# Preparation and attention as one unrolled program, with paired query tiles and an AV product shared by four heads

## The reference, cut to what matters

```
x = x + _layernorm(attention(_layernorm(x)))
x = x + _layernorm(moe(_layernorm(x)))

q = (x @ Wq.T) as 16 heads of 128;  k, v = 4 heads of 128 each
q, k = rope(q), rope(k);  each k and v head serves 4 q heads
scores = q @ k.T / sqrt(128), causal mask, softmax
out = (attn @ v).reshape(B, S, 2048) @ Wo.T
```

## Time and profile before

| what | us |
|---|---|
| median of 3 runs (2512.63 to 2517.93) | 2516.22 |
| span of the profiled execution, first to last instruction | 2515.8 |
| PE busy / weight loads / DVE / ACT / POOL | 2040.1 / 1825.9 / 1578.2 / 1186.3 / 715.7 |
| share of the span: PE / DVE / ACT / POOL | 81% / 63% / 47% / 28% |
| chain that ended last, as far as the page follows it | DVE 2% (the norm of `finish`) |

### The profile page before, as it was taken

One profiled execution on the slowest core, in us unless ns is written; L12 is line 12 of the kernel. 1 busy time (PEld: TensorE's weight loads), 2 busy tenths in 40 slices (PEclk: granted clock), 3 DMA queues, 4 the chain that ended last, 5 costly groups with the idle time before them and its releaser, 6 DMA issues. The chain is left out here.

```text
span 2515.8 us, 46912 instructions
## 1 busy us (share of the span) xinstructions
PE 2040.1 (81%) x15459; PEld 1825.9 (73%) x15459; DVE 1578.2 (63%) x3449; ACT 1186.3 (47%) x2906; POOL 715.7 (28%) x760
## 2 busy tenths in 40 slices
PE   1269999999989999998999999899999747636630
PEld 1159999989879998887899989789998625434420
DVE  5237676766877766688676767876676548810008
ACT  2026566656556666555566656556666411111110
POOL 0012332323323333223333323333333100034542
PEclk9969999999999999999999999999999957756655
DMA  9600101020110001011100020110100022145535
GB/s 371 261 17 26 43 2 43 2 76 18 43 52 26 18 27 40 38 43 51 44 15 29 1 77 18 43 51 26 43 1 1 1 91 74 42 142 130 132 98 183
DMA packets 71749, 153.57 MB, mean 61 GB/s; under 512 B 9496, under 2 KB 52392, under 8 KB 67928
## 3 DMA queue, kind: packets, MB, share of 16 engines
q1 hardware_dynamic: 62840, 126.60, 14.6%
q0 software_dynamic: 8672, 24.02, 3.5%
HBM read 106.34 MB, written 44.26 MB: 60 GB/s over the span
## 5 line engine op out<-in xcount | busy, mean ns | idle before, releaser
L387 PE MATMUL s_ps<-kT,qT 128*128 128x512 f32 (+3 forms) x2304 | 577.0, 367 | 23.3 <-PE prod_ps L353 9.2
L568 ACT ACTIVATE pT<-t_ps 128x512 fp32r<-128x512 f32 (+3 forms) x768 | 349.3, 491 | 390.6 <-PE t_ps L396 387.4
L408 PE MATMUL av_ps<-pT,v 128*128 128x256 f32 (+1 forms) x3840 | 502.3, 283 | 19.8 <-ACT y_part L584 17.0
L408 PEld LDWEIGHTS av_ps<-pT,v 128*128 128x128 f32 x3840 | 472.7, 191 | 34.8 <-issue 18.7
L493 DVE TENSOR_REDUCE neg_max<-s_ps 128x1 f32<-128x128 f32 (+7 forms) x512 | 385.5, 753 | 126.0 <-PE s_ps L387 117.8
L387 PEld LDWEIGHTS s_ps<-kT,qT 128*128 128x128 f32 x2304 | 406.7, 194 | 66.2 <-issue 31.9
L560 ACT ACTIVATE probs<-s_ps,neg_max 128x128 f32<-128x128 f32 (+7 forms) x512 | 381.7, 746 | 120.8 <-DVE neg_max L493 119.5
L500 DVE TENSOR_TENSOR pT<-t_ps,pT 128x512 fp32r<-128x512 f32 (+3 forms) x768 | 400.9, 549 | 25.9 <-ACT pT L568 19.5
L616 POOL TENSOR_TENSOR roped<-rope_c,rope_s 128x256 f32<-128x256 f32 (+1 forms) x192 | 124.2, 647 | 972.6 <-DVE rope_s L483 666.7
L629 POOL TENSOR_TENSOR y<-y,y_part 128x512 f32<-128x512 f32 x224 | 287.9, 1285 | 306.3 <-ACT y_part L584 306.3
L396 PE MATMUL t_ps<-ident,probs 128*128 128x128 f32 x2304 | 342.0, 275 | 7.3 <-DVE pT L500 7.3
(11 more groups left out here) (166 smaller groups left out, 2144.6 us busy)
## 6 DMA issues: line engine op xcount, KB each, us to landing
w_a<-w_split SPq DMA_DIRECT2D x16, 1024.0 KB, 5.4
w_o<-w_split SPq DMA_DIRECT2D x16, 1024.0 KB, 6.6
e_w_in<-in_expert_w SPq DMA_DIRECT2D x8, 1536.0 KB, 7.8
w_split<-w_hl SPq DMA_DIRECT2D x4, 2560.0 KB, 15.3
xT_split<-pre_xT SPq DMA_DIRECT2D x4, 2048.0 KB, 9.7
xT<-xT_split SPq DMA_DIRECT2D x4, 2048.0 KB, 7.9
w_b<-w_split SPq DMA_DIRECT2D x16, 512.0 KB, 4.2
f_m<-sums SPq DMA_DIRECT2D x8, 1024.0 KB, 11.4
```

The costliest lines, as they stand in the source:

```text
L387: last = pe.matmul(out, qT[:, h // 2, a, h % 2, rows], kT[:, group % 2, s, lo:hi], start=(n == 0), stop=(n == 2))
L408: last = pe.matmul(av_ps[:, cols], v[:, group % 2, a, j], pT[:, n % 2, s, j, cols], start=(j == 0 and m == 0), stop=(j == 2 * p + 1 and m ...
L568: act.activation(pT[:, (k // 2) % 2, 0, first:first + count, (k % 2) * P:(k % 2 + 1) * P], t_ps[n % 2][:, 0:count * P].rearrange("p (j n) ...
```

## The change

`prepare` is gone, and with it the two HBM tables. `attention` is one program that is written out for all 16 groups, with no loop. Nothing changes in `route`, `experts` and `finish`, or in how the host lays out the inputs.

- A row is one query tile of one head. Eight rows make a macro: the 4 heads of the big tile 7-m, then the 4 heads of the small tile m (m from 0 to 3). A group has 4 macros, the program 64 and 512 rows. Step s has the scores of row s+1 and the transposes of row s-1; e is s modulo 8.
- q and k are projected with the weights stationary, so that they come out transposed; the q projection takes tiles m and 7-m together (256 columns). The transposes of q and k are gone. In rope, DVE multiplies with cos, ACT copies the two halves of 64 partitions crosswise out of the bank (`rope_swap`), POOL multiplies them with sin and adds; then ACT copies the high part and POOL subtracts for the low one.
- v is projected with x stationary, 128 columns at a time.
- Each row is scaled by the inverse of its sum before it is transposed (reciprocal on DVE, `scale` on POOL, in place); the copy with a scale behind the output projection is gone. There are 3 buffers for rows, before 4.
- The product with v takes the 4 heads of a tile at once (512 columns moving), and the output projection sums the 4 heads in PSUM; DVE adds the result to y (before ACT and POOL).
- x, the weights and the tables of cos and sin are transposed or split on chip by units inside this program. One PSUM bank, `misc_ps`, serves the units of x, q, k, v and out; `begin_misc` makes PE wait until the unit before has been read.
- The last stage of each norm runs on POOL, and the stages lie at fixed steps.

```diff
-STEPS = GROUP * NT
-BODY = KV_HEADS * STEPS
-PAIRS = BODY // 2
-ROT = 32
+MACROS_PER_GROUP = NT // 2
+GROUPS = B * KV_HEADS
+MACROS = GROUPS * MACROS_PER_GROUP
+ROWS = MACROS * 2 * GROUP
...
-def prepare(nc, x, wpack, consts, w_split, xT_split, rows, sums):
...
+def row_tile(r):
+    m = (r // 8) % MACROS_PER_GROUP
+    return big_tile(m) if r % 8 < GROUP else m
...
+def before_transposes(s):
+    m8, e = divmod(s, 8)
+    if s >= 0 and e == 1 and m8 >= 1:
+        return [("av", 2 * m8 - 1, 2)]
+    if s >= 0 and e == 2 and m8 + 1 < MACROS:
+        return [("q", m8 + 1, 0)]
+    return []
+
+
+def after_transposes(s):
+    if s < 0:
+        return []
+    macro, e = divmod(s, 8)
+    g, m = divmod(macro, MACROS_PER_GROUP)
+    b = g // KV_HEADS
+    there = macro < MACROS
+    out = []
+    if e == 4 and macro + 1 < MACROS:
+        out.append(("q", macro + 1, 1))
+    if e == 1 and there and g % KV_HEADS == 2 and b + 1 < B:
+        out.append(("xt", b + 1, m))
+    if e in (0, 3) and macro >= 1:
+        out.append(("out", 2 * macro - 2 + e // 3, 0))
+    if e in (5, 7) and there:
+        out.append(("av", 2 * macro, (e - 5) // 2))
+    if e == 6 and g + 1 < GROUPS:
+        out.append(("k" if m < 2 else "v", g + 1, m % 2))
+    return out
+
+
+def units_at(s):
...
+            def begin_misc(unit):
+                if not MISC_AT[unit]:
+                    pe.wait_ge(table_read, 4)
+                    return
+                kind, of, n = MISC_ORDER[MISC_AT[unit] - 1]
+                if kind == "xt":
+                    pe.wait_ge(xt_lo, 4 * of + n + 1)
+                elif kind in "qk":
+                    pe.wait_ge(swap_done, ROPE_AT[kind, of, n] + 1)
+                elif kind == "v":
+                    pe.wait_ge(v_lo, V_AT[kind, of, n] + 1)
+                else:
+                    pe.wait_ge(y_done, of + 1)
+
...
+                for h in range(2):
+                    for n, (c, a, s) in enumerate(PASSES):
+                        last = pe.matmul(misc_ps[:, h * 256:(h + 1) * 256], w_q[:, s, half, c, h * HD:(h + 1) * HD],
+                                         pair(xT[:, b % 2, a, c], m), start=(n == 0), stop=(n == len(PASSES) - 1))
...
+                for j in range(begin, end):
+                    for n, (a, s) in enumerate(((0, 0), (0, 1), (1, 0))):
+                        last = pe.matmul(av_ps[:], v[:, g % 2, a, j], pT[:, s, part_slot(p) + j],
+                                         start=(j == 0 and n == 0), stop=(j == blocks - 1 and n == 2))
...
+            for s in range(-1, ROW_STEPS):
+                if s + 1 < ROWS:
+                    scores(s + 1)
+                for u in before_transposes(s):
+                    unit(*u)
+                if 1 <= s <= ROWS:
+                    transpose_probs(s - 1)
+                for u in after_transposes(s):
+                    unit(*u)
...
+            for s in range(-1, ROW_STEPS):
+                if 0 <= s < ROWS:
+                    inverse(s)
+                if s + 1 < ROWS:
+                    row_max(s + 1)
+                if 1 <= s <= ROWS:
+                    probs_low(s - 1)
+                for u in units_at(s):
+                    unit(*u)
+                norm = norm_at(s)
+                if norm and norm[2] < STAT_STAGES:
+                    norm_stage(*norm)
...
+            def rope_swap(kind, of, half):
+                n = ROPE_AT[kind, of, half]
+                act.wait_ge(cos_done, n + 1)
+                act.activation(rope_s[0:64, n % 2], misc_ps[64:128], ACT.Copy)
+                act.activation(rope_s[64:128, n % 2], misc_ps[0:64], ACT.Copy).then_inc(swap_done, 1)
...
+            for s in range(-1, ROW_STEPS):
+                if 1 <= s <= ROWS:
+                    probs_high(s - 1)
+                if s + 1 < ROWS:
+                    exponentials(s + 1)
+                for u in units_at(s):
+                    unit(*u)
+                for u in units_at(s - 2):
+                    if u[0] in "qk":
+                        rope_high(*u)
...
+            def scale(r):
+                pool.wait_ge(inv_ready, r + 1)
+                at = probs[:, r % 3, 0:(row_tile(r) + 1) * P]
+                pool.tensor_scalar(at, at, inv_sum[:, r % 16:r % 16 + 1], None, ALU.mult).then_inc(scaled, 1)
...
+                pool.wait_ge(swap_done, n + 1)
+                pool.tensor_tensor(at, at, table, ALU.mult).then_inc(sin_done, 1)
+                pool.wait_ge(sin_done, n + 1)
+                pool.tensor_tensor(rope_c[:, n % 2], rope_c[:, n % 2], rope_s[:, n % 2], ALU.add).then_inc(rope_done, 1)
...
+            for s in range(-1, ROW_STEPS):
+                if 0 <= s < ROWS:
+                    scale(s)
+                for u in units_at(s - 3):
+                    if u[0] in "qk":
+                        rope_low(*u)
+                for u in units_at(s - 1):
+                    if u[0] in "qk":
+                        rope_add(*u)
...
-    prepare(nc, x, wpack, args, w_split, xT_split, rows, sums)
-    attention(nc, args, x, w_split, xT_split, x1_rows, rows)
+    attention(nc, args, x, wpack, x1_rows, rows, sums)
```

More of the change, by code:

```diff
@@ L182, in attention @@
+V_AT = {u: n for n, u in enumerate([u for u in MISC_ORDER if u[0] == "v"])}
+Y_NORM, X1_NORM, X_NORM = 4, 21, 44
+STAT_STAGES = 9
+def attention(nc, consts, x, wpack, x1_rows, rows, sums):
     with ExitStack() as ctx:
@@ L286, in exists, with tiles @@
[L286 to L300 removed]
+        def tiles(a):
+            return a.rearrange("(t p) n -> p t n", p=P)
@@ new lines, in output @@
+            def output(p):
+                g = p // 8
+                begin_misc(("out", p, 0))
+                pe.wait_ge(av_lo, p + 1)
+                pe.wait_ge(o_lo, g + 1)
+                for h in range(GROUP):
+                    for n, (a, s) in enumerate(((0, 0), (0, 1), (1, 0))):
+                        last = pe.matmul(misc_ps[:, 0:HID], avT[:, a, h], w_o[:, s, h], start=(h == 0 and n == 0),
+                                         stop=(h == GROUP - 1 and n == 2))
+                last.then_inc(out_ready, 1)
@@ new lines, in unit @@
+            def unit(kind, of, n):
+                if kind == "xt":
+                    transpose_x(of, n)
+                elif kind == "q":
+                    project_q(of, n)
+                elif kind == "k":
+                    project_k(of, n)
+                elif kind == "v":
+                    project_v(of, n)
+                elif kind == "av":
+                    attend(of, n)
+                else:
+                    output(of)
+            pe.wait_ge(ident_in, 16)
+            pe.wait_ge(tables_in, 32)
@@ L667 @@
+            for s in range(ROW_STEPS, B * BATCH_STEPS + X_NORM):
+                norm = norm_at(s)
+                if norm and norm[2] >= STAT_STAGES:
+                    norm_stage(*norm)
+            pool.wait_ge(zeros_out, 16 * (B + 3))
 TRASH = 48
```

979 lines of the change are left out of this document (466 added, 513 removed).

## The result

The changed kernel takes 2684.19 us (median of 4 runs, 2681.69 to 2687.02) against 2515.15 us for the kernel before in the same runs (2512.63 to 2517.93): the ratio is 1.067, 95% interval 1.0654 to 1.0685. It is 6.7% slower; I had forecast 2421 us and a range up to 2530.

A forecast was written before the change was run, and what follows sets the result against it. PE was taken as the bound: start 67 us, filling 5, 64 macros of 27.8 (1779, bank stall included), stalls 23 + 10 + 20, tail 34, unchanged stages 481.8, in all 2420 of span, so 2421 us; range 2287 to 2530.

The forecast's parts named there:

- the price of POOL's scaling: POOL's scaling of rows, 4608 columns a macro: 0.82 ns a column, 5.3 us; 11.3 us as the upper end.
- Even at 11.3 the scaled row comes before PE wants it: PE's stall for scaled rows, with scaling at 11.3 us a macro: under 0.2 us for the slowest, row 2.
- The bank: Output projection needs `misc_ps`, filled by the q unit; PE stands 2.1 us a macro for ACT's crosswise copy, 134 us.
- my chain in step 3: From the small part's v product to the crosswise copy: 8.1 us on ACT and DVE against 6.0 of PE's work.
- Rival 1: The one bank of the units costs nothing, PE has no stall before the output: 2287 us; 20%.
- Rival 2: POOL becomes the bound, row scaling queued with rope; decides from 3.4 ns a column, 2682 us at 4 ns; 10%.
- the list of signs: What the trace would show for each case; idle time before L336, ending with POOL's L664, meant POOL as the bound.
- the first scores: End of the start: first scores at 67 us, before at 168.
- the x units: 12 units of x, in step 1 of some macros, make the next q unit wait: 1.9 us each, 23 us.
- PE's busy time in attention: PE busy in attention for about 1650 to 1680 us, against 1753 before.
- The tail: Norms and stores behind the last batch: 34 us, as long as before.
- the small stalls: In attention: 5 us for filling, 10 for norm stages on DVE, 20 for what the list leaves out.

The follow-up runs named there:

- experiment 1: Changed kernel without the reciprocal and the scaling, the transposes waiting on the exponential alone: 2458.37 us, ratio 0.977.
- experiment 7: Changed kernel with POOL scaling a tile that nobody reads, just as long and at the same place, the transposes waiting for the exponential: 2563.87 us.
- experiment 8: Changed kernel with transposes one step later and a fourth buffer of probabilities: 2869.45 us with two units in one step, 2597.72 us with the units spread.
- experiment 2: Changed kernel with the scaling moved from POOL to DVE, 2625.83 us, or to ACT, 2589.09 us.
- experiment 9: Changed kernel with later transposes in balanced order, the rotation's low part on DVE and the output projection in the AV product's bank: 2579.55 us.
- second kernel of experiment 5: Changed kernel without reciprocal and scaling, and with the output projection in the AV product's bank instead of `misc_ps`: 2415.82 us, ratio 0.961.
- first kernel of experiment 10: Changed kernel with no row scaled, DVE multiplying the AV product by transposed reciprocals, and the output projection in the AV product's bank: 2598.39 us.

## Why the prediction was wrong

**The step that failed is the price of POOL's scaling, and the sentence built on it.** The trace had no row for it; I took 0.82 ns a column from a one-input copy and held the two-input sum, 2.13, for the upper bound. It measured 2.5 and 0.28 us a piece, above both: 13.8 us a macro instead of 5.3. "It has one tensor input, so I take the first" was the error: the row's other operand is a scalar for each partition, and nothing in the trace said that such an instruction is as fast as a copy. POOL's other work was right, 26.0 - 13.8 = 12.2 us a macro against 12.5. The Trainium skill ("GPSIMD Engine Reference", section "4.1 Engine selection") calls one-input operations roughly line-rate on GPSIMD; here this one was slower than a two-input one. The trace agrees with its other half, that elementwise work belongs on VectorE: 2846 ns against 938 for 1024 columns.

**"Even at 11.3 the scaled row comes before PE wants it" failed too,** and not by the price alone. It put the wait at under 0.2 us for the slowest row; in the changed kernel it is 235.4 us, 136 times 1.7. The working has no term for what stands ahead of a row in POOL's queue: the small row at 1016.95 stood there for 5.5 us behind the rotation and a weight split, and PE idled 3.1. I had summed these, 12.5 us a macro, as load only. On DVE the scaling took 5.6 us a macro, near my price for POOL, and the kernel still took 2626 us; but there it stands in DVE's queue, and no run has POOL scale at the price that I forecast, so what the price alone cost stays open.

**What a wait costs was priced at the wait.** Waiting for POOL is 235.4 us, but PE also needed 91 us more for the same matmuls, 78 of them by the lower clock (the estimate in experiment 1). At the wait shown the clock went from 1.00 to 0.60 behind 3.06 us of idling. The Trainium skill ("TensorE: Matmul & The Clock Gate", section "What's actually happening") has the clock fall to half when the engine has been idle; the trace agrees, and 0.98 against 0.94 is the mean over the stage. I knew a cold price from the start (2.6 us an x unit) and used none in the loop.

**Where the 226 us come from:** 105 with the load, POOL's scalings and DVE's reciprocals, even if no transpose waits for its results (experiment 7), 120 more when the transposes wait for them. A step of slack with another order of the units recovers 86 (experiment 8), other engines 58 and 95 (experiment 2). These are differences of single edits and don't add up, as experiment 9 shows.

**The bank** (134 us) was the right mechanism at the right place, with a third of the size. The waits L363 <- L552 stand at 31.5 us in the changed kernel, hidden by those for POOL, and at 74.4 once the scaling is gone (62 times, at most 1.2 us, where I had 64 times 2.1), 86 with the issue part. Removing the bank is worth 26 and 43 us. So my chain in step 3 came out 0.8 to 0.9 us too long; which of its links overlap was not traced. Rival 1, 2287 us, had a free bank, and falls even without the scaling: that kernel takes 2416.

**Rival 2** had nearly the number (2682 us) and the place (idle time before L336, ended by L664, as the list of signs said), for partly another reason. It was to decide from 3.4 ns a column, when POOL's macro is as long as the loop. At 2.5 POOL is idle for a fifth of the stage, and it decides all the same, because it is late at particular steps. That threshold was of throughput; the waits in the trace come from lateness at single steps. That its 2682 lies so near the measured 2684 is luck. I gave it 10%.

**Right:** the first scores (67, measured 68.0); the x units (1.9 each and 23 us, measured 12 waits, at most 1.9, 22.0 us); the other stages (481.8 and 481.5). **Sizes off:** PE's busy time in attention, forecast at 1650 to 1680 and 1787 in the changed kernel; only where it stalls least does it come near, 1683 at a clock of 0.99 in the second kernel of experiment 5. The tail is 44 us from the last output part at 2158.3, not 34. The norm's application moved to POOL, "from 2.7 us on DVE to 3.3 on POOL", takes 1.22 us for each of 8 tiles, 9.8 us (min, median and max in ns):

```profile
L710 POOL TENSOR_SCALAR xw<-xb,mv,rstd x32: 1216/1224/1237, 714.9 to 2197.3; 128x256 f32<-128x256 f32 x32
```

The forecast without the failed step can be checked against experiment 1: I had 1837 us for attention, it took 1862. PE's work was 51 us more than I counted (1696 against 1645), the bank 48 less (86 against 134), and the small stalls (46 of them for DVE's low parts) 23 more (58 against 35); 2421 against 2458 in all, with a tail that is 11 us longer.

**Open:** how much of the clock's loss belongs to which wait, as no run changes the clock alone, and why it differs between kernels of equal idle time (below); what all scaling on ACT would take with the free bank, which was not run; the balanced order without the later transposes, which was not run either.

## What to carry to other kernels

An operation on an engine and in a form for which the trace has no row has no upper bound in the trace either: leave the range open on that side, or measure that one form first. Where work enters a chain between two steps of a program whose queues are in order, compare what it takes, with all that stands ahead in its queue, to the shortest step; a busy share of 80% said nothing here. In an order by hand with one row of lookahead, look at how the long units are spread over the steps: two in one step instead of one in each cost 272 us here, with the same work.

## What the runs showed of the hardware

- POOL's product with a scalar for each partition takes 0.28 us and 2.5 ns a column of fp32 (604 ns at 128 columns to 2846 at 1024), longer than its product of two tensors (1285 ns at 512, against 1564). Its subtract-and-multiply with two such scalars takes 1222 ns at 256 columns, its one-input copy 612 at 512.
- The same scaling takes 1154 ns on ACT for 1024 columns and 938 on DVE on average. On DVE it depends on POOL (experiment 2): with POOL idle it takes 288 ns at 128 columns, 486 at 512 and 754 at 1024, which is 0.22 us and 0.52 ns a column; with POOL busy for over nine tenths of that time 847, 1332 and 1241. Nothing here shows which other DVE instructions this holds for: its low parts of 512 transposed probabilities, read out of PSUM, took 683 ns in the kernel before and 685 with the scaling on DVE.
- PE's granted clock in attention was 0.99 with 135 us of idle time (without scaling, free bank) and 0.94 with 305. But idle time alone doesn't set it: it was 0.99 with 246 us in the first kernel of experiment 10 and 0.93 with 241 in the one that scales on DVE.
